# Group averages by lane shuffles on VectorE, one expert's product added by DMA, and a new order on ScalarE, in a kernel of two convolutions with group norms

## The reference

```python
x = x + L0(gn(x))     # dynamic convolution
x = x + conv3x3(gn(x), sign(W))
# L0(v): routing = sigmoid(mean_hw(v) @ w_route.T + b_route)      # one weight per image and expert
#        y = sum over 4 experts of routing[b, e] * conv3x3(v, w_experts[e])
#        silu(batchnorm(y))
```

## Time and profile before

| | before |
|---|---|
| median of 3 runs | 272.66 us (272.64 to 272.78) |
| the profiled execution's own time | 272.72 us |
| its span, first to last instruction | 270.6 us |
| PE, matrix products | 263.6 us busy |
| DVE | 254.6 us busy |
| ACT | 213.0 us busy |
| POOL | 45.5 us busy |
| granted TensorE clock | 1.00 of full speed over the span |
| DMA | 35.20 MB |

### The profile page before, as it was taken

How to read it: one execution, slowest core, us unless ns; L and a number is a source line. 1 busy time by engine, 2 the same in 40 slices (tenths; PEclk the granted TensorE clock), 3 DMA queues, 4 the chain that set the end, 5 groups by cost and what they waited for, 6 DMA issues and landing times.

```text
span 270.6 us, 4214 instructions
## 1 busy us (share of the span) xinstructions
PE 263.6 (97%) x1339; PEld 182.5 (67%) x1339; DVE 254.6 (94%) x461; ACT 213.0 (79%) x469; POOL 45.5 (17%) x61
## 2 busy tenths in 40 slices
PE   8899999999999999999999999999999999999993
PEld 7554857668595766759486776849576675948573
DVE  5799999999999999999999999999999999995984
ACT  2798898898979787997979798897979796736860
POOL 2012120313121120312112021212112021210120
PEclk9999999999999999999999999999999999999999
DMA  6998945552617355452726456261735536272407
GB/s 202 417 388 279 325 150 156 78 155 32 127 78 131 104 79 155 58 134 54 145 80 97 136 79 159 27 128 80 125 108 80 157 47 128 70 136 87 78 2 155
DMA packets 10245, 35.20 MB, mean 130 GB/s; under 512 B 1264, under 2 KB 1904, under 8 KB 10224
## 3 DMA queue, kind: packets, MB, share of 16 engines
q0 software_dynamic: 4176, 15.21, 33.1%
q1 hardware_dynamic: 5616, 19.34, 19.1%
q10 hardware_dynamic: 432, 0.39, 0.4%
HBM read 11.34 MB, written 16.25 MB: 102 GB/s over the span
## 4 chain that ended last, share of the span: by engine, by line
PE 95%; DVE 2%; issue 1%; POOL 0%; ACT 0%; DVEq 0%; POOLq 0%
PE pc L599 43%; PE pa L562 14%; PE pb L562 14%; PE pe_ L562 14%; PE pd L552 6%; PE pd L488 2%; PE ps L531 1%; PE ps L535 1%; DVE U L1178 0%; PE pa L636 0%; PE pb L636 0%; DVE X L1404 0%; PE pc L521 0%; POOL rstd L446 0%; DVE sums L1386 0%
## 5 line engine op out<-in xcount | busy, mean ns | idle before, releaser
L1188 DVE SCALAR_TENSOR_TENSOR U<-we,route,U 128x1152 f32<-128x1152 f32 x45 | 63.7, 1415 | 0.5
L599 PE MATMUL pc<-lo,ws 128*128 128x496 f16 (+3 forms) x270 | 62.0, 375 | 0.0
L599 PE MATMUL pc<-hi,ws 128*128 128x496 f16 (+3 forms) x270 | 59.8, 375 | 0.1
L599 PEld LDWEIGHTS pc<-hi,ws 128*128 128x128 f16 x270 | 26.4, 98 | 29.6 <-issue 0.5
L599 PEld LDWEIGHTS pc<-lo,ws 128*128 128x128 f16 x270 | 27.7, 106 | 26.3
L446 POOL TENSOR_TENSOR rstd<-ve,nhalf 128x2 f32<-128x2 f32 (+1 forms) x19 | 17.5, 923 | 141.4 <-ACT ve L856 120.1
L562 PE MATMUL pa<-V,UM 128*128 128x256 f32 (+1 forms) x180 | 40.7, 375 | 0.0
L562 PE MATMUL pb<-V,UM 128*128 128x256 f32 (+1 forms) x180 | 40.6, 375 | 0.0
L562 PE MATMUL pe_<-V,U 128*128 128x256 f32 (+1 forms) x180 | 40.5, 375 | 0.0
L562 PEld LDWEIGHTS pb<-V,UM 128*128 128x128 f32 x180 | 34.1, 190 | 5.5 <-issue 0.7
L562 PEld LDWEIGHTS pe_<-V,U 128*128 128x128 f32 x180 | 34.2, 190 | 3.9
(11 more groups left out here) (168 smaller groups left out, 400.9 us busy)
## 6 DMA issues: line engine op xcount, KB each, us to landing
X<-x SPq DMA_DIRECT2D x15, 512.0 KB, 5.6
out<-X SPq DMA_DIRECT2D x15, 512.0 KB, 2.6
out<-ev POOLq DMA_DIRECT2D x15, 512.0 KB, 5.5
X<-y POOLq DMA_DIRECT2D x14, 512.0 KB, 4.5
we<-w_experts SPq DMA_DIRECT2D x2, 768.0 KB, 8.2
ws_raw<-w_sign SPq DMA_DIRECT2D x1, 576.0 KB, 10.4
we<-w_experts SPq DMA_DIRECT2D x1, 512.0 KB, 6.2
out<-X SPq DMA_DIRECT2D x1, 384.0 KB, 3.0
```

The source lines that it names most:

```text
L599: mm = mm_(rows[:, r0 - first // W:r1 - first // W, c0:c1], ws[:, tap * C:(tap + 1) * C], plane((hi, lo)[part], i)[:, r0 + ky - 1:r1 + ky ...
L1188: v.scalar_tensor_tensor(out=nine(U[i % RING]), in0=expert(e), scalar=route[:, i, e:e + 1], in1=nine(U[i % RING]), op0=ALU.mult, op1=ALU.a ...
```

## The change

1. **Group averages by shuffles.** For the chains 4 to 17 PE's product `group_stats` goes. DVE gets `group_sums`: it shuffles the columns of `stats` by lane p ^ 1, adds, shuffles the sums by p ^ 2 and adds again, so that each lane has its group's sum in `gsum`. ACT reads `gsum` with a factor of 1/4 where it read PSUM, and a small activation `middle_mean` writes the middle mean by itself. In DVE's queue the shuffles stand behind `inner_rows`; in iteration 15 ahead of `sign_points`.
2. **Expert 1 by DMA.** From image 3 on ACT writes expert 1's product into `scaled` (`scale_second`, behind `mix`), and POOL adds it to `U` by a DMA (`add_scaled`, behind `residual`). DVE's `mix(i, 1)` goes for these images; `mix(i, 2)` waits for the DMA.
3. **ACT's order.** `evacuate(t - 2)` now comes ahead of `variances`; `bias`, `split_hi` and `split_hn` come ahead of `deviation`, `pooled_plane`, `centring` and `pads`.
4. **The high part in halves** for every image (before: for image 0 alone). PE's first half waits for the first half alone.
5. **DVE's order.** `low_part` comes ahead of `pool_routes`; in iteration 1 `mix(2, 1)` comes behind the inverse.
6. **Image 0 in halves.** silu, its sum and the residual are done by half image; the residual stands ahead of image 2's rows. The signs of the weights are taken in two parts, before `variance(2)` and between the halves of silu.

The core of the diff (semaphores, buffers and the counts that follow from them left out):

```diff
+        def first_mix(i):
+
+            return 2 if i >= SCALED_FROM else 1
...
+        def by_shuffles(c):
+
+            return LAG < c < CHAINS - 1
+
+        def group_means(c, a, b):
+
+            return (gsum[:, c, a:b], 1.0 / GSIZE) if by_shuffles(c) else (gstats(c, a, b), 1.0)
...
+            def add_scaled(i):
+                pool.wait_ge(mix_first, firsts_before(i) + 1)
+                pool.wait_ge(scaled_ready, i - SCALED_FROM + 1)
+                g.dma_start(flat(U[i % RING][:]), scaled[:], accum_op=ALU.add).then_inc(scaled_added, 16)
...
                 if ND <= t < B and t not in DVE_RESIDUAL:
                     residual(t)
+                if t + LAG - 1 < B:
+                    add_scaled(t + LAG - 1)
...
             def route_logits(i):
                 pe.wait_ge(pooled_ready, i + 1)
+                if i == LAG:
+                    pe.wait_ge(centre_ready, 2 * i)
+                    pe.wait_ge(dev_ready, i)
+                if i > LAG:
+                    pe.wait_ge(th_ready, i)
...
-                    pe.wait_ge(hi_ready, 1 if i == half == 0 else his(i))
+                    pe.wait_ge(hi_ready, his(i) - (half == 0))
...
                     if t > 1:
-                        group_stats(c)
                         sign_half(t - 2, 1, 1, TAP_ORDER[-1:])
...
+            def middle_mean(c):
+                activation(gmid[:, c:c + 1], gsum[:, c, MID:MID + 1], ACT.Copy, scale=1.0 / GSIZE) \
+                    .then_inc(gmid_ready, 1)
...
+            def scale_second(i):
+
+                wait(act, scaled_added, 16 * (i - SCALED_FROM))
+                activation(scaled[:].rearrange("p (g n) -> p g n", n=C), expert(1), ACT.Copy,
+                           scale=route[:, i, 1:2]).then_inc(scaled_ready, 1)
...
+            def first_silu(half):
+
+                act.wait_ge(bn_ready, 5)
+                act.wait_ge(direct_ready, half + 1)
+                activation(flat3(y[0][:])[:, half * BANK:(half + 1) * BANK], direct_bank(0)[:, half, :], ACT.Silu,
+                           bias=bn_shift[:, 0:1], scale=bn_direct[:, 0:1],
+                           accum_out=(ysum[:, 0:1], first_ysum[:])[half]).then_inc(silu_ready, 1)
...
-                for first, last in ((0, H // 2 + 1), (H // 2 + 1, H)) if i == 0 else ((0, H),):
+                for first, last in ((0, H // 2 + 1), (H // 2 + 1, H)):
...
+            sign_weights(0, 4)
             variance(2)
...
-            sign_weights()
-            silu(0)
-            mean_mid(0)
+            first_silu(0)
+            first_half_mean()
+            sign_weights(4, K * K)
+            first_silu(1)
+            first_mean()
...
                 if t > 1:
                     var_mid(t - 1)
                     add_variance(c, MID)
+                    evacuate(t - 2)
                 variances(c)
                 if t > 1:
+                    middle_mean(c)
                     copy_minus(t)
-                    evacuate(t - 2)
+                bias(c, MID)
+                split_hi(t - 1)
+                split_hn(t - 1)
                 deviation(c)
                 if c < B:
+                    pooled_plane(c)
                     centring(c)
                     pads(c)
-                bias(c, MID)
-                split_hi(t - 1)
-                if c < B:
-                    pooled_plane(c)
-                split_hn(t - 1)
...
                 if c < B:
                     routing(c)
                     mix(c)
+                    scale_second(c)
...
+            def group_sums(c):
+
+                a, step = 0, 1 if c < B else 3
+                data = stats[:, c, 0:4:step]
+                if c < B:
+                    dve.wait_ge(nm_in_ready, c + 1)
+                dve.wait_ge(nm_mid_ready, c - LAG + 1)
+                dve.wait_ge(spread_ready, columns_to(c))
+                for n, bit in enumerate((1, 2)):
+                    source = (data, pairs[:, 0:4:step])[n]
+                    target = (pairs[:, 0:4:step], gsum[:, c, 0:4:step])[n]
+                    wait(dve, pairs_ready, c - LAG - 1 + n)
+                    v.stream_shuffle(swapped[:, n, 0:4:step], source, [p ^ bit for p in range(32)]) \
+                     .then_inc(swapped_ready, 1)
+                    dve.wait_ge(swapped_ready, 2 * (c - LAG - 1) + n + 1)
+                    op = v.tensor_tensor(target, source, swapped[:, n, 0:4:step], ALU.add)
+                    op.then_inc((pairs_ready, gsum_ready)[n], 1)
...
                 if t == B - 1:
+                    group_sums(t + LAG - 1)
                     sign_points()
+                if t == 1:
+                    first_residual()
                 all_rows(t + 1)
-                if t == 1:
-                    residual(0)
                 inner_rows(t + 1)
+                if 1 < t < B - 1:
+                    group_sums(t + LAG - 1)
                 transform_minus(t + 1)
                 transform_plus(t + 1)
                 transform_ends(t + 1)
-                mix(t + 1, 1)
+                if t > 1:
+                    mix(t + 1, 1)
                 inverse_sums(t)
                 inverse_inner(t)
                 inverse_outer(t)
+                if t == 1:
+                    mix(t + 1, 1)
+                low_part(t - 1)
                 pool_routes(t + LAG - 1)
-                low_part(t - 1)
```

More of the change, by code:

```diff
@@ L58 @@
 RING = 3
+SCALED_FROM = 3
 QUARTERS = 4
@@ L282, in mixes_before @@
         def mixes_before(t):
-            return len(DIRECT_PARTS) * (E - 1) * min(t, ND) + (E - 1) * rank(t)
+            return len(DIRECT_PARTS) * (E - 1) * min(t, ND) + sum(E - first_mix(i) for i in range(ND, t))
+        def first_mix(i):
+            return 2 if i >= SCALED_FROM else 1
         def firsts_before(t):
@@ L353, in h_before @@
         def h_before(i):
-            return sum(1 for j in DVE_RESIDUAL if j < i)
+            return sum(2 if j == 0 else 1 for j in DVE_RESIDUAL if j < i)
         def wait_h(eng, i):
-            if i == B - 1:
+            if i in (0, B - 1):
                 eng.wait_ge(h_ready, h_before(i) + 2)
@@ L829, in deviation @@
                     act.wait_ge(nm_in_ready, c + 1)
-                    activation(dev[:, c:c + 1], gnm(c, IN), ACT.Identity, bias=nm(c, IN), scale=-1.0) \
+                    mean, share = group_means(c, IN, IN + 1)
+                    activation(dev[:, c:c + 1], mean, ACT.Identity, bias=nm(c, IN), scale=-share) \
                         .then_inc(dev_ready, 1)
@@ L841, in variance, with wait_group @@
                 last = c == CHAINS - 1
-                act.wait_ge(gvar_ready, c + 1)
+                act.wait_ge(gvar_ready, LAG + 2 if last else c + 1)
                 activation(ve[:, c, k:k + 1], gvar(c, k), ACT.Identity, bias=epsilon[:, last:last + 1],
                            scale=1.0 / (HW * (LAST_SCALE if last else ACT_SCALE) ** 2)).then_inc(ve_ready, 1)
+            def wait_group(c):
+                if by_shuffles(c):
+                    act.wait_ge(gsum_ready, c - LAG)
+                else:
+                    act.wait_ge(gvar_ready, c + 1)
             def variances(c):
                 a, b = cols(c)
-                act.wait_ge(gvar_ready, c + 1)
-                activation(gdev2[:, c, a:b], gstats(c, a, b), ACT.Square, bias=base[:, 0:1]).then_inc(gdev2_ready, 1)
+                wait_group(c)
+                means, share = group_means(c, a, b)
+                activation(gdev2[:, c, a:b], means, ACT.Square, bias=base[:, 0:1],
+                           scale=share).then_inc(gdev2_ready, 1)
                 act.wait_ge(gdev2_ready, c - LAG + 1)
@@ L917, in mix_first_part, with sign_weights @@
                            scale=route[:, i, 0:1]).then_inc(mix_first, 1)
-            def sign_weights():
+            def sign_weights(first, last):
                 act.wait_ge(ws_loaded, 16)
-                activation(ws[:], ws_raw[:], ACT.Sign).then_inc(ws_ready, 1)
+                activation(ws[:, first * C:last * C], ws_raw[:, first * C:last * C], ACT.Sign).then_inc(ws_ready, 1)
             def copy_minus(t):
@@ L1292, in inverse_outer, with first_residual @@
                          .then_inc(y_ready, 1)
-            def residual(i):
-                dve.wait_ge(silu_ready, silus(i))
-                v.tensor_tensor(img(i), flat3(y[i % 2][:]), img(i), ALU.add).then_inc(h_ready, 1)
+            def first_residual():
+                for half in range(2):
+                    dve.wait_ge(silu_ready, half + 1)
+                    part = slice(half * BANK, (half + 1) * BANK)
+                    v.tensor_tensor(img(0)[:, part], flat3(y[0][:])[:, part], img(0)[:, part], ALU.add) \
+                     .then_inc(h_ready, 1)
             def residual_last():
```

74 lines of the change are left out of this document (49 added, 25 removed).

## The result

The changed kernel takes 276.45 us (median of 4 runs, 275.87 to 276.96) against 272.72 us (272.64 to 273.04) for the kernel before in the same runs: a ratio of 1.0138 [1.0125, 1.0151]. It is 3.7 us slower. The forecast was 274.6 us, so 1.9 us slower; the sign is right, and the loss is twice the forecast's. The profiled execution is the slowest of the four, 276.96 us; its span is 275.2.

A forecast was written before the change was run, and what follows sets the result against it. PE bound the kernel at 15.504 us a period; ACT would become the bound at 15.74. From 272.72, -0.48 at the start, +2.60 over 11 periods and -0.24 after image 12 gave +1.88: 274.6 us, range 271.2 to 277.0.

The forecast's parts named there:

- The sum of ACT's round: ACT's work without waits plus all added terms and waits per period: 15.74 us, against PE's 15.39 and 15.504 before.
- the shuffle wait: ACT, per period, waiting for DVE's shuffles and adds of the group sums: 0.05 us, bounds 0 and 0.4.
- the power wait: ACT, per period, idle before the bias until POOL's power ends: 0.53 us, bounds 0.16 to 1.13.
- The sum of the start: First period: PE can start image 1's high part at 50.84 instead of 51.32, 0.48 us sooner.
- the last stage is unchanged: End of the kernel: no time change, because its waits are for PE's products.
- the -0.24 after image 12: After image 12 the delay stays, and two group products still go from PE: 0.24 us saved.
- deviation to its reader: ACT, per period: deviation now right ahead of its reader, 0.28 instead of 0.14, with the semaphore's way: 0.16 us.
- sum with 13.43: 13.43 us is ACT's work without waits in a period before the change; the added terms bring it to 15.74.
- PE as the bound: Rival: ACT's round is 15.39 or less, group products and about 0.5 at the start are gained: 270.5 us; chance 0.13.
- The late DMA: Rival: expert 1's DMA lands after DVE wants it, needing over 9 us against 5.1; chance 0.02.
- The likeliest case: ACT becomes the bound with a round of 15.57 to 15.9, time 272.7 to 276.4 us; chance 0.50.
- Held, or slow: Rival: power held by DVE's transforms, or slow shuffles; round 15.9 or more, 276.4 us and up; chance 0.16.

The follow-up runs named there:

- the repeated run: The changed kernel as it is, run once more: 276.18 us, 1.0121 of the kernel before.
- the filled one: Changed kernel with deviation and centring moved on ACT ahead of the bias, into the wait for the power: 270.79 us, 0.9914 of the kernel before.

## Why the prediction was right or wrong, point by point

The mechanism held: ACT becomes the bound, by its own queue, and its work is that of the list. What failed is the size of the sums. The sum of ACT's round gave 15.74, the rows say 15.86: the shuffle wait was taken at 0.05 and measured 0.20, and the reading of the group sums from SBUF was put at nothing and measured 0.18; the power wait, 0.53 taken and 0.34 measured, hid more than half of that. The sum of the start gave -0.48 at image 1 and -0.17 was measured. A pause of 0.36 in one period was not in the forecast at all. And "the last stage is unchanged" and the -0.24 after image 12 did not hold: image 14 is at +3.52 where image 12 was at +3.57, and the last stage adds 0.16. Of the 1.9 us between forecast and result, some 0.3 is the start, 0.8 the longer round, 0.36 the pause and 0.4 the end.

Steps measured against the list, per period (the numbers are of the two timelines of ACT, and after):

| term | forecast | measured | from |
|---|---|---|---|
| scaling | 1.16 | 1.15 | 124.46 - 123.31 |
| halves | 0.27 | 0.28 | 1.43 - 1.15; 0.28 by the whole high part |
| middle mean | 0.14 | 0.10 | 128.23 - 128.13 |
| deviation to its reader | 0.16 | 0.17 | 132.26 - 131.95 - 0.14 |
| power wait | 0.53 | 0.34 | 129.06 - (128.23 + 0.58 - 0.09) |
| shuffle wait | 0.05 | 0.20 | 127.09 - 125.98 - 0.91 |
| variances, and the bias to `hi`, longer | 0 | 0.18 | 1.04 - 0.92 and 0.33 - 0.27 |
| sum with 13.43 | 15.74 | 15.85 | the rows say 15.86 |

**The shuffle wait** was mis-sized, 0.20 for 0.05. The four steps themselves took 0.75 (126.30 to 127.05), where the dependent products of the earlier trace rows gave 0.76; what the step "0.8 with the way in and out" got wrong was the way in, 0.23 from the column's end to the first shuffle, so the whole way is 0.98. By the estimate that the prediction draws from the Trainium skill's row for shuffles (VectorE: DVE Perf Modes, the perf-mode tier table), each would take 0.27; they took 0.15 to 0.16, so the nearest row was the better guide.

**A term was missing**: ACT now reads the group sums in SBUF, where it read PSUM. `gdev` took 0.30 instead of the 0.26 of the earlier trace rows and of the version with the product on PE, the bias 0.29 instead of 0.24 (0.26 in that version). That is 0.03 to 0.05 an instruction, and 0.18 a period on the steps that I can compare. The Trainium skill, VectorE: DVE Perf Modes, the section on the TRN2 errata, states 224 cycles at 1.2 GHz for a ScalarE operation that reads SBUF and 172 for one that reads PSUM, an estimate of 0.043 us apart: the rows agree. I had costed "where it read PSUM" in the list of changes at nothing.

**The power** was the largest term too high, by 0.19, and softened the error: it took 0.72 at its new place, not 0.92. The rival in which the power is held longer behind the shuffles went the wrong way in the steady state (the last section shows why). This was luck as much as judgement: in each period the power starts 0.14 to 0.16 us before the end of the transform `V<-f_rows` that DVE runs, and in the version without the DMA adds one that started 0.14 before it was held by the next transform and took 1.32.

Together the round came out at 15.86, 0.12 over the 15.74. Over eleven periods that would be 1.3 us; there were ten, as the start below shows. The **pause of 0.36** in one period, which no row of before could show, comes on top.

**The start** was the other mis-sized step: -0.48 was forecast at image 1, -0.17 came (the two halves of the forecast, image 0's edits and the move of `mix(2, 1)`, were measured apart above). Image 0's high part did start 0.60 sooner. What the forecast lacked was the price of moving `mix(2, 1)`: it took that as free. On DVE the product comes later, and with it image 2's kernel rows, for which PE waits 0.39. It also lacked the profit of that move, that the power is no longer held (1.12 in the first period before, 0.70 after), without which image 0's halves would have gained nothing. On the other hand the ACT-bound pace began only at image 2, not at image 1, so that there were 10 slow periods, not 11.

With these the sum closes on the table: -0.30 at image 2, +0.29 in the first slow period, 9 x 0.356 = 3.21 in the others and 0.36 for the pause are +3.56, against +3.57 at image 12. With -0.05 to image 14 and 0.16 in the last stage it is 3.7: the span of the repeated run is 3.7 longer, and the medians of the result lie 3.7 apart.

**The rivals.** PE as the bound (270.5) is what the version without scaling (270.44) and the filled one (270.79) give: the price of that case was right, the case was not the change's own. The late DMA fell: 5.2 us to landing against the 5.1 by bytes, and without it the same round. The likeliest case asked for a round of 15.57 to 15.9 and 272.7 to 276.4 us: the round of 15.86 lies in it, near its end, and the time just above it. "Held, or slow" forecast 276.4 and up at a round of 15.9: the time landed there, but by the shuffles' way in, SBUF reads, the pause and the end, not by a held power.

## What to carry to other kernels

Cost a change on the queue that will bound the kernel, not on the one that bounds it now, and include what each small instruction reads from and how a semaphore's way in adds to a chain of short steps. Where a queue must wait for another engine, put its cheap work that is wanted late into that wait: here two small steps ahead of the bias turned a loss of 1.2% into a gain of 0.9%. When parts of a change look separable, test what one needs of another: the shuffles without the moved product lost 1.7%, and the moved evacuation without the shuffles 3.6%.

## What the runs showed of the hardware that I had not expected

**A GpSimd power that VectorE holds ends a fixed time after VectorE's instruction.** In 23 of the 26 two-column powers of before and after, the power ends 0.56 to 0.58 us after the end of the DVE instruction that was running when it started; it lasts 0.72 to 1.16 us accordingly. The twelve of after, all 0.72, say little by themselves, since a power beside an idle DVE takes 0.71; the eleven of before, 0.80 to 1.16, carry the reading. Two pairs of before, DVE and POOL:

```profile
32.28 1.41 DVE L1188 SCALAR_TENSOR_TENSOR U<-we,route,U 128x1152 f32<-128x1152 f32 x1
...
124.35 0.69 DVE L1257 TENSOR_TENSOR V<-e_rows 128x512 f32<-128x512 f32 x1
```

```profile
33.13 1.12 POOL L446 TENSOR_TENSOR rstd<-ve,nhalf 128x2 f32<-128x2 f32 x1 [11.12 <-ACT ve L856]
```

The product ends at 33.69, its power at 34.25, 0.56 later; the transform ends at 125.04, the power of the earlier trace rows at 125.62, 0.58 later. With DVE idle, as in each period of the version with the product on PE, it takes 0.71. Where the power starts within about 0.1 us of the DVE instruction's end, the next DVE instruction can be the one it waits for: 1.94 beside the product, 1.24 beside `V<-e_rows`. The line is not sharp: with 0.14 left one power was held by the next instruction (1.32) and others were not (0.72), and one power of before was held by the next although 0.34 was left (1.52 at 47.19). Why is open. That next one did not hold it where it read one operand from PSUM (`sums<-pa,minus`, beside the power of 0.70 at 32.76). This agrees with the Trainium skill, SBUF — State Buffer, SBUF: two separate sides: a VectorE instruction with two inputs in SBUF and a GpSimd instruction that reads SBUF exclude each other, and the second blocks until the first is through. The runs show it one way only: a power under way did not hold the product that DVE started beside it (1.41 us from 124.95, while the power of the earlier trace rows runs until 125.62; away from a power this product takes 1.41 to 1.42 too). My error was to apply it as "more transforms beside it, so longer": what counts is how much is left of one DVE instruction at the power's start. At its old place 0.22 to 0.59 was left in the middle periods, at the new one 0.14 to 0.16, so that the power is hardly held at all.

**Two shuffles and two adds of four columns** over groups of four lanes took 0.75 us, each step 0.19 to 0.20 from start to start, and 0.98 from ACT's column to the sum. The load of the mask is recorded at 0.01 us and took no time of its own apart from the one pause of 0.36, whose cause stays open. Where PE is the bound the pause costs nothing (the high parts of the filled version stay 15.37 apart across it); with the evacuation back, or the high part whole, it costs the same 0.36.

**A DMA that adds 576 KB from SBUF to SBUF** every period left the round unchanged at 15.86, and the time within what these runs can tell (276.20 without it, 276.18 with it).
